# Attention on one core: values' low parts beside the high ones, and the two halves of the output bank added by VectorE

## The chip, the cores and the metric

One core of a Trainium2 chip runs the whole program. TensorE multiplies (PE in the profile; PEld is its weight load), ScalarE (ACT) and VectorE (DVE) empty the eight accumulation banks, GpSimd (POOL) works between on-chip tiles, SyncE's queue (SP) issues transfers. The metric is the device time in microseconds: 1926.93 us is the median of 3 runs of the kernel before (1922.9 to 1926.97).

## The reference, cut to what matters

The program is a small decoder on 2 batches of 512 tokens of width 512. Six stages follow each other: causal attention with 16 heads of 32 (`a0`), attention to a memory, a mixture of experts, rotary causal attention with 32 query heads and 8 key/value heads of 64 (`a1`), linear attention, and a second mixture. Only the two attentions change:

```
def _L0_attn_ref(x, Wq, Wk, Wv, Wo):            # NH = 16, hd = 32
    att = jnp.einsum('bhtd,bhsd->bhts', q, k) / jnp.sqrt(hd) + mask   # causal
    w = jax.nn.softmax(att, axis=-1)
    z = jnp.einsum('bhts,bhsd->bhtd', w, v)
    return z.transpose(0, 2, 1, 3).reshape(B, T, D) @ Wo.T

def _L1_attn_ref(x, w_in, w_out, rms_w):        # 8 groups of 4 heads, DQK = DV = 64
    q, k = _rope(q), _rope(k)
    attn = jax.nn.softmax(where(causal, qk, -inf), axis=-1)
    o = jnp.einsum('bghsp,bgxpd->bghsd', attn, v)
    return x + jnp.einsum('bsc,mc->bsm', o, w_out)
```

## The kernel before

**Precision.** Every f32 operand is held as two fp32r parts: a high part (ScalarE's rounding copy) and a low part (what VectorE or GpSimd gets by subtracting it, helper `low_part`, lines 158 to 165). A product is three passes of fp32r matmuls, high by high, high by low, low by high (helper `product`, line 153). The part low by low is left out.

**Slots.** Both attentions are one class, `Attention`. Each runs 4 steps of 128 output columns. In `a0` a step has 8 jobs (2 batches, 4 heads); in `a1` 16 (2 batches, 4 query tiles, 2 heads). A job is one head's softmax(QK)V over 512 tokens. The loop variable `m` counts slots, and each engine walks over them in its own order, which the program writes out by hand; semaphores tie them together. In slot `m` TensorE does the scores of job `m`, the transposes of the normalised weights of job `m-2`, a "fill", then the values of job `m-3` (`_pe_values`). VectorE does the masking and maximum of job `m` (line 836), the reciprocal of job `m-1` (line 842), the rotary work, the low part of job `m-2`'s transposed weights (`a_PHL`, three instructions on line 165), and its share of the fill.

**Fill.** The table `FILL` says which piece of a projection goes in a slot: `P` a projection of 12 matmuls, `T` the turning of the values, `O` a tile of the output product. In `a1` the fills repeat every 8 slots. I number them 0 to 7: P, P, P, OO, P, OO, P (of the values), T+P. An O of `a1` is 12 matmuls, one of `a0` 3. In `a0` 4 slots repeat, 0 to 3: P+OO, P, P, OOT. The first O of a slot 3, and of slot 7 in `a0`'s count of 8, reads the attention outputs of the job whose values were computed in the slot before.

**Rotary chain of `a1`.** A projected tile is emptied by ScalarE into `a_f` (line 809), turned by 4 transfers into `a_g` (line 669), multiplied by GpSimd (line 700) and VectorE (881), added (884), rounded (768), its low part taken (first instruction after the reciprocal two slots later, line 164 or 165), and moved by 4 transfers (line 654) into the operands of the scores. There are two `a_f`/`a_g` pairs, so the next projection but one waits for those moves.

**Output bank.** Bank 7 (`OB`) accumulates the values of all heads of a tile: 4 jobs in `a0`, 2 in `a1`. `VH` and `VL` hold the values' parts, head by head, each in its own columns of 128 with zeros elsewhere, so a head's product lands in its own partitions. After the last head ScalarE copies the bank into `QH` (line 759) and VectorE writes bank minus `QH` into `QL` (the end of its slot), both 128 partitions. `QL` then frees the bank and lets the O products start.

## Time and profile before

| | |
|---|---|
| median of 3 runs | 1926.93 us |
| profiled execution | 1936.33 us, of it span 1934.9 us |
| `a0`'s slots | about 40 to 245 us of the span |
| `a1`'s slots | about 979 to 1494 us |
| busy in the span | PE 94%, PEld 81%, DVE 58%, ACT 42%, POOL 52% |
| granted clock | 0.98 of 2.4 GHz |

A stretch of the page is only as slow as the wait that ends last in it, so the busy shares over the span say little about two stages that together fill some 37% of it (`a0`'s 205 us and `a1`'s 515 us of 1934.9). What is needed is which engine TensorE waits for inside a slot.

### The profile page before, as it was taken

How to read it: one execution, taken by the hardware profiler on the slowest of the kernel's cores; microseconds unless marked ns; L12 is line 12 of the kernel's file. 1: busy time of each engine (PE TensorE's matmuls, PEld its weight loads, DVE VectorE, ACT ScalarE, POOL GpSimd, SP SyncE). 2: the span in 40 equal slices, each digit the busy share in tenths (PEclk: the TensorE clock that was granted, in tenths of full speed). 3: DMA queues.
4: the chain of work that ended last, by engine and by line, in shares of the span. 5: the costliest groups of instructions: out<-in, count | busy, mean ns of one | idle time of the engine just before them, and what ended most of it. 6: DMA issues, size and time to landing. Idle time of an engine off the chain costs nothing.

```text
span 1934.9 us, 30810 instructions
## 1 busy us (share of the span) xinstructions
PE 1813.6 (94%) x10167; PEld 1568.5 (81%) x10167; DVE 1116.9 (58%) x2769; ACT 804.9 (42%) x2063; POOL 1009.1 (52%) x965
## 2 busy tenths in 40 slices
PE   7999989989799999999889999999999999999896
PEld 5888867778799999898668888888888888867795
DVE  6667785663233333335766666666665757566344
ACT  3766633222122222221257556665564433543231
POOL 3444342487773957895456556455453203116783
PEclk9999999999899999999999999999999999999998
DMA  3556430156553545544343243233321210012655
GB/s 116 171 154 202 138 136 35 58 182 220 179 181 132 197 161 179 188 153 118 90 115 93 66 105 103 56 89 98 80 69 55 73 50 1 24 49 98 207 199 191
DMA packets 104552, 232.54 MB, mean 120 GB/s; under 512 B 20673, under 2 KB 20929, under 8 KB 101329
## 3 DMA queue, kind: packets, MB, share of 16 engines
q1 hardware_dynamic: 84080, 144.31, 24.7%
q0 software_dynamic: 19744, 85.47, 13.4%
q8 instruction: 90, 1.47, 0.3%
q10 hardware_dynamic: 576, 0.79, 0.2%
q14 instruction: 62, 0.50, 0.1%
HBM read 126.23 MB, written 57.93 MB: 95 GB/s over the span
## 4 chain that ended last, share of the span: by engine, by line
PE 55%; DVE 5%; POOL 4%; issue 3%; DMA 3%; SPq 3%; ACT 2%; another core or an unknown queue 1%; POOLq 0%; DVEq 0%; ACTq 0%
PE bank L153 45%; PE bank L1025 2%; PE bank L1009 2%; PE bank L2188 2%; PE bank L2179 2%; SPq L669 1%; DMA a_g<-a_f 1%; POOL a_g L700 1%; SPq L654 1%; DMA a_QL<-a_g 1%; POOL f_UL L165 1%; POOL a_E L706 1%; DVE X L1894 1%; PE bank L2940 1%
## 5 line engine op out<-in xcount | busy, mean ns | idle before, releaser
L706 POOL TENSOR_SCALAR a_E<-a_E,a_inv 128x128 f32<-128x128 f32 (+3 forms) x384 | 222.1, 596 | 219.9 <-DVE a_inv L842 219.9
L153 PE MATMUL bank<-f_UH,f_XH 128*128 x596 | 200.8, 337 | 22.9 <-POOL f_UL L165 12.3
L739 ACT ACTIVATE a_E<-a_E,a_top 128x512 f32<-128x512 f32 (+3 forms) x384 | 211.1, 567 | 5.1 <-DVE a_top L836 5.0
L153 PE MATMUL bank<-f_UH,f_XL 128*128 x596 | 193.6, 325 | 0.0
L153 PE MATMUL bank<-f_UL,f_XH 128*128 x596 | 193.5, 325 | 0.0
L731 ACT ACTIVATE a_PHL<-bank 128x512 fp32r<-128x512 f32 (+1 forms) x288 | 131.0, 528 | 133.1 <-PE bank L1025 133.0
L153 PE MATMUL bank<-a_PHL,a_VH 128*128 128x512 f32 (+3 forms) x768 | 180.4, 324 | 0.3 <-DVE a_QL L165 0.3
L836 DVE CUSTOM_DVE_ANT_0 a_E<-a_causal,bank 128x512 f32<-128x512 bf16 (+3 forms) x384 | 163.8, 482 | 28.0 <-PE bank L1009 16.2
L1837 DVE TENSOR_TENSOR f_gate<-bank,f_gate 128x352 f32<-128x352 f32 x79 | 41.4, 525 | 206.6 <-PE bank L153 180.5
L165 DVE TENSOR_TENSOR a_PHL<-bank,a_PHL 128x512 fp32r<-128x512 f32 (+1 forms) x288 | 153.8, 588 | 10.1 <-ACT a_PHL L731 10.0
L1782 ACT ACTIVATE f_HH<-bank 128x256 fp32r<-128x256 f32 x220 | 59.9, 324 | 239.5 <-PE bank L2179 211.9
L700 POOL TENSOR_TENSOR a_g<-a_g,a_cos_sin 128x512 f32<-128x512 f32 x40 | 68.7, 1718 | 158.8 <-DMA a_g<-a_f 158.8
L153 PE MATMUL bank<-f_DH,f_HH 128*128 (+1 forms) x330 | 139.5, 423 | 9.9 <-issue 5.5
L153 PEld LDWEIGHTS bank<-a_PHL,a_VH 128*128 128x128 f32 x768 | 134.8, 189 | 14.3 <-DVE a_QL L165 0.6
L165 POOL TENSOR_TENSOR f_UL<-f_uraw,f_UH 128x2816 fp32r<-128x2816 f32 (+1 forms) x27 | 141.5, 5242 | 2.3
L1025 PE MATMUL bank<-ident,a_E 128*128 128x128 f32 x960 | 127.7, 278 | 14.9 <-DVE a_PHL L165 11.1
L153 PEld LDWEIGHTS bank<-f_UH,f_XH 128*128 128x128 f32 x596 | 113.4, 190 | 25.1 <-issue 25.1
L153 PE MATMUL bank<-f_DH,f_HL 128*128 (+1 forms) x330 | 131.6, 399 | 0.0
L153 PE MATMUL bank<-f_DL,f_HH 128*128 (+1 forms) x330 | 131.0, 397 | 0.0
L165 POOL TENSOR_TENSOR f_DL<-f_draw,f_DH 128x1024 fp32r<-128x1024 f32 (+1 forms) x54 | 98.3, 1839 | 61.4 <-DVE f_row L217 59.3
L1771 ACT ACTIVATE f_gate<-bank 128x352 f32<-128x352 f32 x110 | 51.2, 466 | 184.0 <-PE bank L153 151.1
L1025 PEld LDWEIGHTS bank<-ident,a_E 128*128 128x128 f32 x960 | 108.9, 142 | 21.7 <-DVE a_PHL L165 13.2
(407 smaller groups left out, 4954.3 us busy)
## 6 DMA issues: line engine op xcount, KB each, us to landing
f_uraw<-f_up POOLq DMA_DIRECT2D x18, 1408.0 KB
f_xb<-table SPq DMA_DIRECT2D x86, 256.0 KB
table<-f_ob SPq DMA_DIRECT2D x86, 256.0 KB
table<-a_zeros SPq DMA_DIRECT2D x31, 512.0 KB, 3.9
f_draw<-f_down POOLq DMA_DIRECT2D x27, 512.0 KB
a_g<-a_f SPq DMA_DIRECT2D x160, 64.0 KB, 2.0
a_raw<-a_qkv SPq DMA_DIRECT2D x36, 256.0 KB
f_uraw<-f_up POOLq DMA_DIRECT2D x9, 704.0 KB
```

What stands on the lines that cost most here:

```text
L153: m = pe.matmul(out, a, b, start=first and i == 0 and j == 0, stop=last and i == n - 1 and j == 2, skip_group_check=not check)
L165: return dve.tensor_tensor(lo, src, hi, ALU.subtract)
L700: e.tensor_tensor(g, g, self.cos_sin[:, 1, :], ALU.mult).then_inc(*self.s_p2.up(N, *x))
L706: e.tensor_scalar(self.E[sl][:, a], self.E[sl][:, a], self.inv[:, sl, i:i + 1], 0.0, ALU.mult, ALU.add).then_inc(*self.s_nrm.up(N, m - 1, i))
L731: e.activation(self.PH[m % 2][:, at:at + size], bank[:, 0:size], ACT.Copy).then_inc(*self.s_phi.up(N, m - 2, ci))
L739: x = e.activation(E, E, ACT.Exp, scale=-1.0, bias=self.top[:, sl, i:i + 1], accum_out=self.total[:, sl, i:i + 1])
L836: e.tensor_tensor_reduce(self.E[sl][:, self.E_AT[i]:self.E_AT[i] + w], self.causal[:, T - w:T], bank[:, off:off + w], -1.0, HUGE, ALU.add, ...
L1009: t = e.matmul(bank[:, off:off + w], (self.QH, self.QL)[h][:, r, qs], keys[:, h, ks], start=x == 0, stop=x == 1)
L1025: t = e.transpose(self.k.bank[bk][:, at:at + P], self.E[sl][:, self.E_AT[i] + sblk * P:self.E_AT[i] + (sblk + 1) * P], self.k.ident[:, :])
L1771: e.activation(self.gate[:, :], bank[2 + n % 2][:, 0:INNER], ACT.Silu).then_inc(*self.s_gate.up(N, n))
L1782: m = e.activation(self.HH[ps, cs, :], src, ACT.Copy)
L1837: e.tensor_tensor(self.gate[:, :], bank[4 + n % 2][:, 0:INNER], self.gate[:, :], ALU.mult).then_inc(*self.s_hid.up(N, n))
```

## The change

1. `VH` and `VL` become one tile `V`: a head's low part sits in the same 128 columns, 64 columns away from the high part. One pass then gives high-by-x in the head's own half of the bank's partitions and low-by-x in the other half. The values take two passes (`V` by `PH`, `V` by `PL`) instead of three. Low by low is now included.
2. The bank holds one half's heads at a time, so it closes after 2 jobs in `a0` and after every job in `a1`, and every opening waits until VectorE has emptied it.
3. Emptying is three instructions on 64 partitions: ScalarE copies the own half to `QH`; VectorE writes `S` = other half minus `QH` (the bank is read 64 partitions away from where `S` is written), waits for itself, and writes `QL` = own half plus `S`.
4. VectorE does this one slot later than before, behind the maximum and the reciprocal of the new slot.
5. `a0`'s fill puts `T` ahead of the two `O`. The clearing of `V` at the start falls from two tiles to one in `a0`, to none in `a1`.

```diff
@@ -439,7 +439,8 @@
         else:
             self.KH, self.KL = sb("KH", [heads, NTOK], F32R), sb("KL", [heads, NTOK], F32R)
             self.cos_sin = sb("cos_sin", [2, T])
-        self.VH, self.VL = sb("VH", [heads, NT, P], F32R), sb("VL", [heads, NT, P], F32R)
+        self.V = sb("V", [heads, NT, P], F32R)
+        self.S = sb("S", [T])
         self.E = [sb(f"E{i}", [1280]) for i in range(self.SLOTS)]
         PHL = sb("PHL", [4, 1280], F32R)
         self.PH, self.PL = [PHL[:, i, :] for i in range(2)], [PHL[:, 2 + i, :] for i in range(2)]
@@ -459,9 +461,9 @@
         if rotary is None:
             self.FIRST = [[("P", K, 0)], [("P", 0, 0)], [("P", V, 0)], [("T", 0)]]
             self.FILL = [[("P", K, 1), ("O", 2, -1), ("O", 3, -1)], [("P", 0, 1)], [("P", V, 1)],
-                         [("O", 4, -1), ("O", 5, -1), ("T", 1)],
+                         [("T", 1), ("O", 4, -1), ("O", 5, -1)],
                          [("P", K, 0, 1), ("O", 6, -1), ("O", 7, -1)], [("P", 0, 0, 1)], [("P", V, 0, 1)],
-                         [("O", 0), ("O", 1), ("T", 0, 1)]]
+                         [("T", 0, 1), ("O", 0), ("O", 1)]]
             self.SPLIT = {2: (K, 1), 3: (0, 1), 5: (V, 1), 6: (self.wt, 0)}
             self.LEAD = {K: 3, 0: 4, V: 2, self.wt: 2}
             self.NORM = {-2: [4, 5], -1: [6, 7]}
@@ -594,9 +596,9 @@
                 for i in range(TT):
                     self.s_nrm.plan((N, m, i))
                 self.s_av.plan((N, m))
-                if h == self.heads - 1:
-                    self.s_ohi.plan((N, j, r, b))
-                    self.s_olo.plan((N, j, r, b))
+                if self.closes(h):
+                    for s in (self.s_ohi, self.s_olo):
+                        s.plan((N, j, r, b, self.half(h)))
     def moves(self, j, c, b):
@@ -613,6 +615,25 @@
                     [(self.QL[up, c, a], f[dn, :]), (self.QL[dn, c, a], g[dn, :])]]
         return [[(self.KH[up, 0, a], g[up, :]), (self.KH[dn, 0, a], g[up, :]), (self.KL[up, 0, a], f[up, :])],
                 [(self.KH[up, 1, a], g[dn, :]), (self.KH[dn, 1, a], g[dn, :]), (self.KL[dn, 1, a], f[dn, :])]]
+    def half(self, h):
+        return h * self.hd // self.HALF
+    def opens(self, h):
+        return h * self.hd % self.HALF == 0
+    def closes(self, h):
+        return (h + 1) * self.hd % self.HALF == 0
+    def low_columns(self, cs):
+        at = (cs.start + self.HALF) % P
+        return slice(at, at + self.hd)
+    def halves(self, h):
+        own = slice(self.half(h) * self.HALF, (self.half(h) + 1) * self.HALF)
+        return own, slice((1 - self.half(h)) * self.HALF, (2 - self.half(h)) * self.HALF)
     def out_weights(self, x, r):
         return x[:, self.wt + r, :, :].rearrange("p k n -> p (k n)")
@@ -679,8 +700,8 @@
         else:
             e.memset(self.KL[:, :, :].bitcast(F32), 0.0)
         e.memset(self.causal[:, :], 0.0).then_inc(*self.k.g.up())
-        for z in (self.VH, self.VL):
-            e.memset(z[:, :, :, :].bitcast(F32), 0.0)
+        if 2 * self.hd < P:
+            e.memset(self.V[:, :, :, :].bitcast(F32), 0.0)
         last = self.causal[:, T - P:T]
         e.wait_ge(*self.k.g.now())
         e.affine_select(out=last, in_=last, compare_op=ALU.is_ge, fill=MASKED, base=0, pattern=[[-1, P]],
@@ -753,11 +774,13 @@
                     self.norm.act_tile(i)
             if self.rotary is not None and m == self.VALUES:
                 self._act_rotated(m - 1)
-            if 3 <= m < self.M + 3 and self.jobs[m - 3][3] == self.heads - 1:
+            if 3 <= m < self.M + 3 and self.closes(self.jobs[m - 3][3]):
                 j, b, r, h = self.jobs[m - 3]
+                own, other = self.halves(h)
+                bank = self.k.bank[self.OB]
                 e.wait_ge(*self.s_av.after(N, m - 3))
-                e.activation(self.QH[:, r, b * T:b * T + T], self.k.bank[self.OB][:, :], ACT.Copy).then_inc(
-                    *self.s_ohi.up(N, j, r, b))
+                e.activation(self.QH[own, r, b * T:b * T + T], bank[own, :], ACT.Copy).then_inc(
+                    *self.s_ohi.up(N, j, r, b, self.half(h)))
     def _act_rotated(self, m):
@@ -840,6 +863,8 @@
                 sl = (m - 1) % self.SLOTS
                 e.wait_ge(*self.s_ex.after(N, m - 1, 2))
                 e.reciprocal(self.inv[:, sl, :], self.total[:, sl, :]).then_inc(*self.s_inv.up(N, m - 1))
+            if 4 <= m < self.M + 4 and self.closes(self.jobs[m - 4][3]):
+                self._dve_low_values(m - 4)
             if self.rotary is not None:
                 for x in self.projected(m - 2):
                     s = self.slot[x]
@@ -859,12 +884,17 @@
                 self.norm.dve_second()
             for i in self.NORM.get(m, []):
                 self.norm.dve_rest(i)
-            if 3 <= m < self.M + 3 and self.jobs[m - 3][3] == self.heads - 1:
-                j, b, r, h = self.jobs[m - 3]
-                a = slice(b * T, b * T + T)
-                e.wait_ge(*self.s_ohi.after(N, j, r, b))
-                low_part(e, self.QL[:, r, a], self.k.bank[self.OB][:, :], self.QH[:, r, a]).then_inc(
-                    *self.s_olo.up(N, j, r, b))
+    def _dve_low_values(self, m):
+        e, N, (j, b, r, h) = self.k.dve, self.name, self.jobs[m]
+        (own, other), a, key = self.halves(h), slice(b * T, b * T + T), (N, j, r, b, self.half(h))
+        bank = self.k.bank[self.OB]
+        e.wait_ge(*self.s_ohi.after(*key))
+        e.tensor_tensor(self.S[own, :], bank[other, :], self.QH[own, r, a].bitcast(F32), ALU.subtract).then_inc(*self.k.d.up())
+        e.wait_ge(*self.k.d.now())
+        e.tensor_tensor(self.QL[own, r, a], bank[own, :], self.S[own, :], ALU.add).then_inc(*self.s_olo.up(*key))
     def _stats(self, loaded, tiles):
@@ -901,7 +931,7 @@
                 src, bs = bank[:, :].rearrange("p (i c) -> p i c", i=TT), slice(b * TT, b * TT + TT)
                 e.wait_ge(*self.s_vhi.after(N, j, b))
                 for h, cs in self.head_rows:
-                    i = low_part(e, self.VL[:, h, bs, cs], src[:, :, cs], self.VH[:, h, bs, cs], scale=1.0)
+                    i = low_part(e, self.V[:, h, bs, self.low_columns(cs)], src[:, :, cs], self.V[:, h, bs, cs], scale=1.0)
                 i.then_inc(*self.s_vlo.up(N, j, b))
             else:
                 _, j, g = x
@@ -979,7 +1009,7 @@
                 if g == 0:
                     e.wait_ge(*self.s_wlo.after(N, j, self.wt + Q - 1))
                 if g % TT == 0:
-                    e.wait_ge(*self.s_olo.after(N, j, self.queries[-1], g // TT))
+                    e.wait_ge(*self.s_olo.after(N, j, self.queries[-1], g // TT, self.half(self.heads - 1)))
                 a = slice(g * P, g * P + P)
                 product(e, bank[:, :], [(self.QH[:, r, a], self.QL[:, r, a]) for r in range(Q)],
                         [(self.out_weights(self.WH, r), self.out_weights(self.WL, r)) for r in range(Q)]).then_inc(
@@ -1033,19 +1063,18 @@
         j, b, r, h = self.jobs[m]
         if r == self.queries[0] and h == 0:
             e.wait_ge(*self.s_vlo.after(N, j, b))
-        if h == 0 and self.OB in emptied:
+        if self.opens(h) and self.OB in emptied:
             e.wait_ge(*emptied[self.OB])
         for ci, chunk in enumerate(self.TCHUNKS):
             e.wait_ge(*self.s_plo.after(N, m, ci))
             for sblk, _ in chunk:
                 a = slice(self.P_AT[sblk], self.P_AT[sblk] + T - sblk * P)
-                t = product(e, self.k.bank[self.OB][:, sblk * P:T],
-                            [(self.VH[:, h, b * TT + sblk, :], self.VL[:, h, b * TT + sblk, :])],
-                            [(self.PH[m % 2][:, a], self.PL[m % 2][:, a])],
-                            first=h == 0 and sblk == 0, last=h == self.heads - 1 and ci == 2)
+                for x, weights in enumerate((self.PH, self.PL)):
+                    t = e.matmul(self.k.bank[self.OB][:, sblk * P:T], self.V[:, h, b * TT + sblk, :], weights[m % 2][:, a],
+                                 start=self.opens(h) and sblk == 0 and x == 0, stop=self.closes(h) and ci == 2 and x == 1)
         t.then_inc(*self.s_av.up(N, m))
-        if h == self.heads - 1:
-            emptied[self.OB] = self.s_olo.after(N, j, r, b)
+        if self.closes(h):
+            emptied[self.OB] = self.s_olo.after(N, j, r, b, self.half(h))
     def projections_done(self):
```

VectorE's order in a slot 3 of `a1` (`a_top` is the running minimum, `a_inv` the reciprocal, `a_f` and `a_g` the rotary tiles). Before:

```order
L884 TENSOR_TENSOR a_f<-a_f,a_g 128x512
L165 TENSOR_TENSOR a_PHL<-bank,a_PHL 128x512 x2
L165 TENSOR_TENSOR a_PHL<-bank,a_PHL 128x256
L165 TENSOR_TENSOR a_QL<-bank,a_QH 128x512
L836 ISA a_E,a_top<-a_causal,bank 128x512
L836 ISA a_top 128x1
```

and, behind that slot's reciprocal:

```order
L842 RECIPROCAL a_inv<-a_total 128x4
L164 SCALAR_TENSOR_TENSOR a_f<-a_f,a_g 128x512
L881 TENSOR_TENSOR a_f<-a_f,a_cos_sin 128x512
L884 TENSOR_TENSOR a_f<-a_f,a_g 128x512
```

The same place in the changed kernel:

```order
L865 RECIPROCAL a_inv<-a_total 128x4
L895 TENSOR_TENSOR a_S<-bank,a_QH 64x512
L897 TENSOR_TENSOR a_QL<-bank,a_S 64x512
L164 SCALAR_TENSOR_TENSOR a_f<-a_f,a_g 128x512
L911 TENSOR_TENSOR a_f<-a_f,a_cos_sin 128x512
L914 TENSOR_TENSOR a_f<-a_f,a_g 128x512
```

What emptied the bank stood ahead of the slot's first maximum; now a pair of instructions stands behind the last one and the reciprocal, ahead of the rotary work, in every slot of `a1` and every second one of `a0`.

TensorE's order in a slot 3 of `a0`, from the transposes to the first values. Before:

```order
L1025 MATMUL bank<-ident,a_E 128x128 x10
L153 MATMUL bank<-a_WH,a_QH 128x512
L153 MATMUL bank<-a_WL,a_QH 128x512
L153 MATMUL bank<-a_WH,a_QL 128x512
L153 MATMUL bank<-a_WH,a_QH 128x512
L153 MATMUL bank<-a_WL,a_QH 128x512
L153 MATMUL bank<-a_WH,a_QL 128x512
L972 MATMUL bank<-ident,a_f 128x128 x4
L153 MATMUL bank<-a_PHL,a_VH 128x512 x2
L153 MATMUL bank<-a_PHL,a_VL 128x512
```

In the changed kernel:

```order
L1055 MATMUL bank<-ident,a_E 128x128 x10
L1002 MATMUL bank<-ident,a_f 128x128 x4
L153 MATMUL bank<-a_WH,a_QH 128x512
L153 MATMUL bank<-a_WL,a_QH 128x512
L153 MATMUL bank<-a_WH,a_QL 128x512
L153 MATMUL bank<-a_WH,a_QH 128x512
L153 MATMUL bank<-a_WL,a_QH 128x512
L153 MATMUL bank<-a_WH,a_QL 128x512
L1073 MATMUL bank<-a_PHL,a_V 128x512 x2
```

The four turnings of the values moved ahead of the two O, and the third pass of the values is gone.

## Rows read from the trace of the kernel before

**Rows 1.** Windows: one 4-slot group of `a0`, two 8-slot groups of `a1`.
```profile
core 0: us, PE busy (x) PEld busy (x) DVE busy (x) ACT busy (x) POOL busy (x), PEclk, DMA share, GB/s
100.55:126.69 26.14, 26.14 (x159) 23.34 (x158) 18.34 (x59) 18.37 (x55) 12.07 (x19) 1.00 0.52 159
1100.50:1165.06 64.56, 62.95 (x367) 55.67 (x365) 43.40 (x121) 39.59 (x110) 33.31 (x41) 1.00 0.34 87
1165.06:1230.40 65.34, 63.13 (x367) 55.64 (x365) 43.52 (x121) 39.72 (x110) 35.74 (x43) 1.00 0.33 85
```

**Rows 2.** Timeline (start us, duration us) of PE, `a1`: one job's values, next scores.
```profile
1105.63 0.62 PE L153 MATMUL bank<-a_PHL,a_VH 128*128 128x512 f32 x2
...
1107.53 0.39 PE L1009 MATMUL bank<-a_KH,a_QL 128*128 128x512 f32 x1
```

**Rows 3.** Timeline of PE, `a1`: slot 3, scores to first output product.
```profile
1121.59 0.39 PE L1009 MATMUL bank<-a_KH,a_QL 128*128 128x512 f32 x1
...
1123.67 0.64 PE L1025 MATMUL bank<-ident,a_E 128*128 128x128 f32 x3 [0.64 <-DVE a_PHL L165]
...
1125.52 0.47 PE L153 MATMUL bank<-a_WH,a_QH 128*128 128x512 f32 x1
```

**Rows 4.** Timeline of DVE in slots 1 to 3 of the same group.
```profile
1111.26 1.79 DVE L881 TENSOR_TENSOR a_f<-a_f,a_cos_sin 128x512 f32<-128x512 f32 x1
...
1116.99 0.65 DVE L164 SCALAR_TENSOR_TENSOR a_f<-a_f,a_g 128x512 fp32r<-128x512 f32 x1
1120.29 0.69 DVE L881 TENSOR_TENSOR a_f<-a_f,a_cos_sin 128x512 f32<-128x512 f32 x1 [2.65 <-DMA a_g<-a_f]
...
1122.94 1.61 DVE L165 TENSOR_TENSOR a_PHL<-bank,a_PHL 128x512 fp32r<-128x512 f32 x3
1124.68 0.69 DVE L165 TENSOR_TENSOR a_QL<-bank,a_QH 128x512 fp32r<-128x512 f32 x1
1125.29 0.68 DVE L836 CUSTOM_DVE_ANT_0 a_E<-a_causal,bank 128x512 f32<-128x512 bf16 x1
...
1127.01 0.66 DVE L164 SCALAR_TENSOR_TENSOR a_f<-a_f,a_g 128x512 fp32r<-128x512 f32 x1
```

**Rows 5.** Timeline of SyncE's queue and ACT: moves and turns, an emptying.
```profile
1111.37 0.50 SPq L654 DMA_DIRECT2D a_QH<-a_g  x1
...
1116.22 2.65 SPq L669 DMA_DIRECT2D a_g<-a_f  x4
1118.93 0.58 SPq L654 DMA_DIRECT2D a_QH<-a_g  x1
...
1115.60 0.60 ACT L809 ACTIVATE a_f<-bank 128x512 f32<-128x512 f32 x1 [1.11 <-DMA a_QL<-a_g]
```

**Rows 6.** Waits, 900 to 1380 us: total, times, longest.
```profile
DVE a_QL L165 <- ACT a_QH L759: 43.0, 21, 3.9
```

**Rows 7.** Timeline of PE and ACT, `a1`, slots 6 and 5.
```profile
1281.23 0.39 PE L1009 MATMUL bank<-a_KH,a_QH 128*128 128x256 f32 x1 [0.63 <-DVE X L913]
...
1148.11 0.63 ACT L781 ACTIVATE a_WH<-a_raw 128x512 fp32r<-128x512 f32 x1 [7.30 <-PE bank L153]
```

**Rows 8.** Timeline of PE and DVE, `a0`: slot 3 from its scores.
```profile
100.55 0.81 PE L1006 MATMUL bank<-a_KS,a_QS 96*128 96x512 f32 x4
...
102.22 0.47 PE L153 MATMUL bank<-a_WH,a_QH 128*128 128x512 f32 x1
...
106.04 0.89 PE L1006 MATMUL bank<-a_KS,a_QS 96*128 96x512 f32 x4
...
101.38 0.69 DVE L165 TENSOR_TENSOR a_QL<-bank,a_QH 128x512 fp32r<-128x512 f32 x1 [3.47 <-ACT a_QH L759]
```

**Rows 9.** Timeline of PE, end of `a1`: a slot without fill, last output product.
```profile
1458.48 0.39 PE L1009 MATMUL bank<-a_KH,a_QH 128*128 128x512 f32 x1
...
1462.79 0.40 PE L1009 MATMUL bank<-a_KH,a_QL 128*128 128x512 f32 x1
...
1493.03 0.47 PE L153 MATMUL bank<-a_WH,a_QH 128*128 128x512 f32 x1 [1.50 <-DVE a_QL L165]
```

More of the change, by code:

```diff
@@ L452, in __init__ @@
                          [self.E[i][:, a * D:(a + 1) * D] for i in range(self.SLOTS) for a in range(2)], rms)
+        self.HALF = P // 2
         self.head_rows = [(h, slice(h * hd, h * hd + hd)) for h in range(heads)]
@@ L796, in _act_fill @@
                 for h, cs in self.head_rows:
-                    i = e.activation(self.VH[:, h, b * TT:b * TT + TT, cs], src[:, :, cs], ACT.Copy, scale=1.0)
+                    i = e.activation(self.V[:, h, b * TT:b * TT + TT, cs], src[:, :, cs], ACT.Copy, scale=1.0)
                 i.then_inc(*self.s_vhi.up(N, j, b))
```

## The prediction, written before the changed kernel ran

> **What bounds the kernel now.** I read the page for the shares, then the windows of the attention stages, then the timelines of TensorE and VectorE over one repeating group of slots, and last those of ScalarE and SyncE's queue where one of the two waited. In a group of 4 slots of `a0` TensorE is busy for all of 26.14 us; in a group of 8 slots of `a1` for 62.95 of 64.56 us and 63.13 of 65.34 [rows 1]. The granted clock is 1.00 there, the level of 2.4 GHz. So TensorE sets the pace, and a pass taken from it is worth its full time wherever nobody else becomes late. VectorE is busy for 43.4 of 64.56 us, but that average hides the place that matters. In slot 3 of `a1` TensorE has the scores at 1121.59 and waits for VectorE's `a_PHL` before its transposes at 1123.67 [rows 3]. VectorE is late there: its maximum starts at 1125.29 [rows 4], 3.7 us behind the scores. It is late because its rotary work waited 2.65 us for a transfer (`a_g`) [rows 4]. The reader is to see that two things run side by side in `a1`: TensorE's stream, and a chain of transfers and VectorE steps that catches up with it once per group.
>
> **What the change removes.** The values of a job take 12 matmuls from 1105.63 to 1107.53, 1.90 us [rows 2]. All passes are alike, so the third of them is 1.90 / 3 = 0.63 us. There are 96 jobs (32 in `a0`, 64 in `a1`): 61 us if all of it counted. The clearing of `V` at the start saves GpSimd time only, ahead of its first weights; the first slots wait for the norm on VectorE, so I put it at nothing.
>
> **What it adds.** VectorE gets 160 instructions in place of 40. One of 512 columns from the bank takes 0.69 us alone and lets the next begin after 0.61 (`a_QL` at 1124.68, the next at 1125.29) [rows 4]. The trace has none on 64 partitions, and none whose input lies in other partitions than its output; the columns are the same 512, so I take the same 0.69. The second waits for the first: 0.69 + 0.03 + 0.69 = 1.41 us to the result, 1.32 until the next instruction. From below, two overlapped instructions would be 0.61 + 0.69 = 1.3. From above, the longest VectorE instruction of 512 columns here is the rotary product at 1111.26, 1.79 us while GpSimd works on the partner tile [rows 4]: twice that is 3.6 us. I take 1.41, since the rows that read the bank are the nearest. ScalarE gets 40 more copies of 0.60 us; it waits 1.11 us in the same slot for a transfer [rows 5], which hides them.
>
> **What it moves.** The old `a_QL` stood at the end of a slot, waiting for ScalarE's copy of values just computed: 43.0 us of waiting in 21 times [rows 6]. That wait goes. The new pair stands behind the maximum and reciprocal. It rarely waits itself, because ScalarE's copy is from the slot before. But three others wait for it. (a) The first O of slot 3 or 7. (b) The next opening of the bank. (c) Everything behind it on VectorE: the low part that releases SyncE's moves, the rotary product, `a_PHL`.
>
> **(a) in `a1`.** `a_PHL`'s three end for the next instruction at 1122.94 + 1.53 = 1124.47; without the old `a_QL` the maxima start there. From 1125.29 to 1127.01 maxima and reciprocal take 1.72 us [rows 4]. Then the pair, 1.41, and 0.15 to reach TensorE (`a_QL` ended at 1125.37, the O began at 1125.52 [rows 3, 4]): 1124.47 + 1.72 + 1.41 + 0.15 = 1127.75, where the O now starts at 1125.52. That is 2.2 us later than before, although TensorE was ready earlier: what it saved in slots 0 to 2 (3 x 0.63) is lost as well, because `a_PHL` hangs on the transfer chain. Other groups give 1.7 to 2.0; I take 1.95. After it the values of slots 3 to 7 save 5 x 0.63 = 3.15. Net per group: 3.15 - 1.95 = 1.2 us.
>
> **(c) in `a1`.** The pair stands before the low part of slot 1 and slot 2. In slot 1 what is removed pays for it: the old instruction, 0.61, and its wait, 43.0 / 21 = 2.0 us on average [rows 6], against 1.32. In slot 2 the low part ended at 1117.6 (started at 1116.99) [rows 4] and would now end at 1118.9. Its move was issued at 1118.93 in any case, since the queue was busy with the turns, 1116.22 + 2.65 = 1118.87 [rows 5]. So the chain isn't late by it, but there is no slack left. If that cover is gone, the chain is 1.3 us longer per group: 10 us over 8 groups. The rotary product of slot 2 waits 2.65 us for its transfer [rows 4], which hides the pair once more.
>
> **One more loss in `a1`.** In slot 5 of every second group ScalarE waits 7.30 us, until TensorE is through with its O, before it rounds new output weights [rows 7]; VectorE's addition to `X` in that slot hangs on it, and the third score matmul group of slot 6 waits 0.63 us for that addition [rows 7]. The shorter values only lengthen this wait: 0.63 lost in those groups.
>
> **(a) in `a0`.** Slot 3 started at 100.55 and took 5.49 us; its O began at 102.22 without waiting, since `a_QL` was early [rows 8]. Now: a 512-column matmul is 512 / 3840 x 1.90 = 0.25 us [rows 2], so the first maximum comes 0.25 + 0.15 = 0.4 us after the scores begin (in `a1`, two passes, 0.65); then 1.72, 1.41 and 0.15: the O at 3.7 us. The two O are 6 x 0.25 = 1.5, the values 1.27: 6.45 instead of 5.5, +0.95. Slots 0 to 2 save 0.63 each (their openings come later in the slot than the pair). Net per group 1.9 - 0.95 = 0.95 us.
>
> **(b) at the ends.** A slot without a P or O has nothing between transposes and values. In `a1` such a slot took 1462.79 - 1458.48 = 4.31 us [rows 9]; now the pair is done 0.65 + 1.72 + 1.41 + 0.15 = 3.9 us after the scores, and with values of 1.27 it takes 5.2: +0.9 each. The last group of `a1` has three of them, then three jobs in which TensorE, ScalarE and VectorE take turns on one bank (values 1.3, copy 0.6, pair 1.4) before the last O, which now starts at 1493.03 [rows 9]. The last group with its end: +1.3 for the O of slot 3, -1.3 for the values of the two slots with O, +2.7 for the three empty ones, +0.7 for the taking turns: +3.4. That of `a0`: +0.95 for slot 3, +1.2 for the empty slot that opens the bank, -1.3 for two that don't, +0.85 in the last two openings: +1.7.
>
> **The sum.** `a0`: first group, three slots at -0.63, -1.9; five groups at -0.95, -4.75; the last with its end +1.7: -4.9. `a1`: first group (no O, bound by the chain but for two slots) -1.3; three groups with the weight wait 3 x (1.2 - 0.63) = -1.7; three without, 3 x 1.2 = -3.6; the last +3.4: -3.2. Together -8.1 us. The profiled execution took 1936.33 us (1934.9 of it span), 9.4 more than the median of the runs. It would take 1928.2, and the median falls from 1926.93 to 1918.8. Of 61 us taken from TensorE, over 50 come back as waits.
>
> **A rule that speaks against the pair.** Successive instructions of VectorE start 0.61 us apart at a duration of 0.69 [rows 4], so they overlap by 0.08. The Trainium skill ("VectorE: DVE Perf Modes", section "Two Vector instructions with no wait between them") says that an instruction is held until all earlier ones have finished when its input starts in another 32-partition group than the last input from that memory. No run here shows this yet. Here it would hold the first of the pair behind the reciprocal, and for the upper half the maximum after it: 0.1 us at each of some 20 places where TensorE waits for the pair. By it the sum is -6.1 instead of -8.1 us.
>
> **Rivals.**
> *Covered.* The old wait of VectorE for ScalarE [rows 6] is what makes it late, and without it VectorE runs ahead: then the O waits 0 to 1 us and the savings of slots 0 to 2 hold. Against it: in slots 1 and 2 the wait is for a transfer [rows 4, 5]. It gives up to 8 x 0.63 - 1.2 = 3.8 us more per group of `a1` and 0.95 of `a0`; with half of the first, in six groups each, 11 + 6 = 17 us more, 25 in all: 1902. With no wait at all, 61 us: 1866.
> *Nothing.* The openings cost in ordinary slots as well: a P slot has scores (1.27), transposes and 12 x 0.25 = 3.0 of projection ahead of its values, over 4.3 us, and the pair at 3.9 if VectorE is on time. When it is a microsecond behind, the values wait too. With 0.5 us in one slot of each of the 16 groups it takes 8 us, the whole gain: 1927.
> *Slower.* The rotary chain. Its place is the low part behind the pair in slots 1 and 2; its price 1.3 us each, where SyncE's queue does not hide it; it decides once the low part is later than the end of the turns, for which there is 0.0 us of slack today [rows 5]. Both in all 8 groups: 8 x 2.6 = 21 us, less 8.1: 1940. It also comes if the pair costs its upper bound (2.2 us more at about 20 places, 44 us: 1963).
> *Not what it says.* If reading across partitions needed another route, VectorE's instruction at L895 would show it as a longer duration; this is part of the case above.
>
> **Chances.** Forecast 0.52; covered 0.17 (of it 0.04 for the full 61 us); nothing 0.13; slower 0.18. A difference of 0.2% (4 us) is about what a measurement of this kernel tells from none. The forecast reaches from 1909 to 1925, by the bounds of the pair (0.1 us of it moves the sum by 2 us) and my reading of one group for all; nearly all of it is faster. From covered 0.17, forecast 0.49 and 0.04 of the others, faster is 0.70; same 0.14; slower 0.16. The range is 1899 to 1933: it leaves out the full gain and most of the slower case.
>
> **What would show it.** TensorE's matmuls of the values: 768, two per width, 1.27 us a job. In slot 3 of both stages a wait of TensorE for L897 ahead of the first O, 1.4 to 2.5 us; in slots 0 to 2 of `a1` no gain, in 4 to 7 0.63 each. L895 and L897 at 0.69 us. VectorE's wait for ScalarE's `a_QH` nearly gone. The group of `a0` at 25.2 us, those of `a1` at 63.4 to 64.8. The forecast is wrong if the groups shrink by 4 us or more (covered), or if moves and turns on SyncE's queue come later than before, measured from the group's start (slower).

## The result: slower by 1.45%

The changed kernel takes 1953.8 us (median of 6 runs, 1945.45 to 1959.1), the kernel before 1926.12 in the same job (6 runs, 1922.9 to 1928.69). The ratio is 1.0145 with a 95% interval of 1.012 to 1.017: 27.7 us slower, where I had forecast 8.1 us faster. The profiled execution took 1954.1 us, only 17.8 more than that of before. The profile of before is slow at its end: from the last O of `a1` to the end of the program, where the code is the same, it took 441.9 us, against 430.9 to 437.9 in the twelve other profiles of this case (433.5 in after). From `a1`'s first scores to its last O the change costs 28.4 us in the profiles, near the 27.7 of the medians.

### The profile page after: what moved, and what is told of

The parts are those of the page before. It is cut to its first block and busy times, and to the rows that moved or that the text cites. A ratio compares the mean times of both kernels' runs of the same rounds, so it can differ in the third digit from the quotient of the medians.

```text
span 1952.8 us, 30233 instructions
## 1 busy us (share of the span) xinstructions
PE 1778.7 (91%) x9777; PEld 1532.4 (78%) x9783; DVE 1211.1 (62%) x2889; ACT 831.5 (43%) x2103; POOL 1009.0 (52%) x962
## 5 line engine op out<-in xcount | busy, mean ns | idle before, releaser
L727 POOL TENSOR_SCALAR a_E<-a_E,a_inv 128x128 f32<-128x128 f32 (+3 forms) x384 | 230.6, 618 | 222.7 <-DVE a_inv L865 222.7
L153 PE MATMUL bank<-f_UH,f_XH 128*128 x596 | 200.9, 337 | 20.2 <-POOL f_UL L165 15.1
L1073 PE MATMUL bank<-a_PHL,a_V 128*128 128x512 f32 (+3 forms) x768 | 141.2, 327 | 14.5 <-DVE a_QL L897 14.5
L1073 PEld LDWEIGHTS bank<-a_PHL,a_V 128*128 128x128 f32 x768 | 128.6, 193 | 31.5 <-DVE a_QL L897 17.0
L153 PE MATMUL bank<-YH,a_WH 128*128 128x512 f32 x288 | 121.4, 421 | 6.3 <-ACT a_f L832 2.3
```

Source lines behind the costliest of these rows:

```text
L153: m = pe.matmul(out, a, b, start=first and i == 0 and j == 0, stop=last and i == n - 1 and j == 2, skip_group_check=not check)
L727: e.tensor_scalar(self.E[sl][:, a], self.E[sl][:, a], self.inv[:, sl, i:i + 1], 0.0, ALU.mult, ALU.add).then_inc(*self.s_nrm.up(N, m - 1, i))
L1073: t = e.matmul(self.k.bank[self.OB][:, sblk * P:T], self.V[:, h, b * TT + sblk, :], weights[m % 2][:, a], start=self.opens(h) and sblk == ...
```

## The profile after

**Stages.** The windows of the kernel after (columns as in [rows 1]): a group of `a0` from slot 3 to slot 3 as in [rows 1], two groups of 8 slots of `a1`, and slots 2 and 3 of the first of them.

```profile
98.27:123.72 25.45, 23.92 (x143) 21.05 (x141) 20.72 (x62) 19.07 (x56) 12.02 (x19) 1.00 0.53 166
1101.85:1170.50 68.65, 61.73 (x334) 53.48 (x333) 53.54 (x133) 41.67 (x113) 34.59 (x41) 0.95 0.33 81
1170.50:1237.25 66.75, 61.76 (x334) 53.63 (x333) 52.46 (x133) 43.16 (x115) 37.25 (x43) 0.95 0.33 83
1117.49:1125.58 8.09, 8.09 (x39) 7.37 (x39) 5.67 (x16) 4.92 (x14) 2.21 (x3) 0.79 0.39 94
1125.58:1140.16 14.58, 11.22 (x53) 9.04 (x51) 11.44 (x23) 5.86 (x15) 7.52 (x10) 0.88 0.44 106
```

The group of `a0` is 25.45 us; counted from slot 0 the regular ones take 25.2 to 25.5 us and one 26.45 (forecast 25.2). Those of `a1` are 68.65 and 66.75 instead of 64.56 and 65.34 [rows 1]; I had said 63.4 to 64.8. The same rows say how the loss is paid. Two passes instead of three save TensorE 8 x 0.63 = 5.06 us in a group. In the first group its idle time grows from 64.56 - 62.95 = 1.6 to 68.65 - 61.73 = 6.9 us, which is +5.3. Its busy time should fall from 62.95 to 57.9 but falls only to 61.73, which is +3.8, at a granted clock of 0.95 instead of 1.00. 5.3 + 3.8 - 5.06 = 4.1, the difference of the two lengths. In the second group: +2.8, +3.7, -5.06, in sum +1.4. So the loss has two parts, waiting and slower work. The slow stretches are slots 2 and 3: 0.79 and 0.88.

For the whole of `a1`, from the start of its first scores to the start of its last O, before and after:

```profile
979.33:1493.03 513.70, 489.44 (x2818) 429.24 (x2816) 340.24 (x960) 311.87 (x868) 269.92 (x337) 0.99 0.33 84
```
```profile
977.12:1519.26 542.14, 474.77 (x2562) 407.50 (x2560) 416.95 (x1056) 333.27 (x901) 279.03 (x337) 0.94 0.31 79
```

Idle time: 24.3 becomes 67.4, +43.1. Busy time: 489.4 less 64 x 0.63 = 40.3 would be 449.1 and is 474.8, +25.6. Sum: 43.1 + 25.6 - 40.3 = 28.4, the difference of the two lengths. The slower work is over a third of what eats the saving.

**Who waits.** The waits of TensorE in that stretch, first after, then before (us in total, times, longest).

```profile
PE bank L153 <- DVE a_QL L897: 17.0, 8, 2.2
PE bank L1039 <- DMA a_QH<-a_f: 14.4, 8, 2.3
PE bank L1055 <- DVE a_PHL L165: 12.0, 8, 2.4
PE bank L1073 <- DVE a_QL L897: 10.1, 8, 2.1
PE bank L1039 <- DVE X L943: 8.7, 6, 2.1
```
```profile
PE bank L1025 <- DVE a_PHL L165: 11.1, 9, 3.1
...
PE bank L1009 <- DMA a_QH<-a_f: 3.3, 2, 2.3
PE bank L153 <- DVE a_QL L165: 2.7, 4, 1.5
PE bank L1009 <- DVE X L913: 1.9, 3, 0.6
```

The first row is the wait I forecast (the O of slot 3 for the pair). The second I did not: the scores of slot 2 now wait in every group for the moved `QH`, before in two. The fourth is the opening of the bank; all but one of its places are in the last group of `a1`. The fifth is slot 6's wait for the addition to `X`. These four grew by 42 us, nearly all of the 43.1.

**TensorE, slots 2 and 3** of the group of rows 3 to 5 (start us, duration us; slot 0 begins at 1101.85).

```profile
1117.49 0.52 PE L1039 MATMUL bank<-a_KH,a_QH 128*128 128x512 f32 x1 [1.70 <-DMA a_QH<-a_f]
...
1119.72 2.00 PE L1055 MATMUL bank<-ident,a_E 128*128 128x128 f32 x10
...
1125.58 0.40 PE L1039 MATMUL bank<-a_KH,a_QL 128*128 128x512 f32 x1
...
1132.00 0.77 PE L153 MATMUL bank<-a_WH,a_QH 128*128 128x512 f32 x1 [2.22 <-DVE a_QL L897]
1132.57 0.63 PE L153 MATMUL bank<-a_WL,a_QH 128*128 128x512 f32 x1
1132.99 0.63 PE L153 MATMUL bank<-a_WH,a_QL 128*128 128x512 f32 x1
...
1135.02 0.40 PE L153 MATMUL bank<-a_WL,a_QH 128*128 128x512 f32 x1
1135.26 0.39 PE L153 MATMUL bank<-a_WH,a_QL 128*128 128x512 f32 x1
```
```profile
1132.00:1134.70 2.70, 2.70 (x7) 2.12 (x7) 2.67 (x3) 0.68 (x4) 2.44 (x3) 0.50 0.69 168
1134.70:1138.90 4.20, 4.20 (x20) 3.48 (x18) 2.56 (x5) 0.63 (x1) 1.92 (x3) 0.98 0.58 141
```

Behind the wait of 2.22 us the O matmuls start 0.43 us apart until 1134.7, at a granted clock of 0.50 (the level of 1.2 GHz), then 0.23 us apart at 0.98 (nearly all at 2.4). Six matmuls lose 0.2 us each. Before, the first O started with no such wait [rows 3]. This is the mildest of such places: from the first to the last of slot 3's 24 O matmuls the seven groups take 6.7 to 8.0 us, six of them before 5.3 and the last 6.0.

**VectorE, slots 1 to 3**, and the transfers and ScalarE's emptying beside it.

```profile
1112.23 0.17 DVE L865 RECIPROCAL a_inv<-a_total 128x4 f32<-128x4 f32 x1
1112.43 0.68 DVE L895 TENSOR_TENSOR a_S<-bank,a_QH 64x512 f32<-64x512 f32 x1
1113.15 0.69 DVE L897 TENSOR_TENSOR a_QL<-bank,a_S 64x512 fp32r<-64x512 f32 x1
1113.87 0.69 DVE L164 SCALAR_TENSOR_TENSOR a_f<-a_f,a_g 128x512 fp32r<-128x512 f32 x1
...
1128.62 0.67 DVE L859 CUSTOM_DVE_ANT_0 a_E<-a_causal,bank 128x512 f32<-128x512 bf16 x1
...
1130.24 0.17 DVE L865 RECIPROCAL a_inv<-a_total 128x4 f32<-128x4 f32 x1
1130.44 0.68 DVE L895 TENSOR_TENSOR a_S<-bank,a_QH 64x512 f32<-64x512 f32 x1
1131.16 0.69 DVE L897 TENSOR_TENSOR a_QL<-bank,a_S 64x512 fp32r<-64x512 f32 x1
```
```profile
1114.59 0.50 SPq L675 DMA_DIRECT2D a_QH<-a_g  x1
...
1120.12 2.67 SPq L690 DMA_DIRECT2D a_g<-a_f  x4
```
```profile
1119.49 0.60 ACT L832 ACTIVATE a_f<-bank 128x512 f32<-128x512 f32 x1 [1.79 <-DMA a_QL<-a_g]
```

Read it as a chain. The low part of slot 1 starts 12.0 us after the group's first scores (1113.87 - 1101.85). Its move is issued the moment it is done, at 12.7, where it was 10.9 before (1111.37 - 1100.50 [rows 1, 5]). In slot 2 the move still waits for the turns on the queue (1120.12 + 2.67), as I had said, so that low part isn't on the chain. The emptying that waits for the moves starts at 17.6 instead of 15.1, the maxima of slot 3 at 26.8 instead of 24.8 [rows 4], and the first O at 30.15 instead of 25.0 [rows 3]. The pair takes 1.64 us from the reciprocal's start to the low part's; without it the low part starts 0.09 us behind the reciprocal.

This group is the latest of the seven that have O products. In five of them the low part of slot 1 starts at 11.3 us (before 10.2 in all seven) and its move is issued at 12.0 (before 10.9), so the wait of slot 2 is there in all. But the maxima of slot 3 come at 25.3 us on average of the seven, after as before. What is late in every group is the O behind them: it starts 3.4 us after the first maximum, since maxima, reciprocal and pair stand ahead of it, where before it started 0.2 to 1.0 us after it. In the six full groups that makes it 3.1 us late on average.

## The experiments

The numbers are medians; each kernel shares its job with runs of the kernel before (1926.78, 1926.46 and 1925.25 us in the three jobs), and the ratio is to those.

**Only `a0`.** In `a1` the values' two tiles, the whole bank and the single instruction at the end of the slot are as before.

```diff
+        self.whole = rotary is not None
     def closes(self, h):
-        return (h + 1) * self.hd % self.HALF == 0
+        return h == self.heads - 1 if self.whole else (h + 1) * self.hd % self.HALF == 0
```

> Only a0 is changed (two passes, pair one slot later, T ahead of the O); a1 is as before. Theory A (the whole loss is in a1, where the pair lengthens the rotary chain): a0 keeps what its slots show, about 5 us, so 1926 - 5 = 1921 (1919 to 1923), and a1 starts earlier but takes its old 64.4 to 65.3 us a group. Rival (the change also costs outside a1, through the tail of the program or SyncE's queue): at or above 1926.

1926.95 us, ratio 1.001 (0.9996 to 1.0025). So the loss is in `a1`. But the 5 us of `a0` aren't there either; see below.

**Low part first.** In `a1` the pair stands behind the rotary low part.

```diff
-            if 4 <= m < self.M + 4 and self.closes(self.jobs[m - 4][3]):
+            mine = 4 <= m < self.M + 4 and self.closes(self.jobs[m - 4][3])
+            if mine and self.rotary is None:
                 self._dve_low_values(m - 4)
             if self.rotary is not None:
                 for x in self.projected(m - 2):
                     ...
+            if self.rotary is not None and mine:
+                self._dve_low_values(m - 4)
```

> The kernel after, but in a1 VectorE writes the rotary low part (which releases SyncE's moves) ahead of the pair instead of behind it; a0 unchanged. Theory A (the pair ahead of the low part lengthens the rotary chain): in slots 1 and 2 the low part comes 1.5 us earlier, the scores of slot 2 no longer wait 1.70 us for a_QH, the maxima and the O of slot 3 come 1.4 to 2.8 us earlier; 1.7 to 2.8 us in each of 8 groups, 14 to 22 us: 1932 to 1940. Rival B (the late first O alone, the pair standing behind the maxima of slot 3): in slot 3 nothing moves, 1952 to 1954. Rival C (TensorE's clock falls after waits): half of A's gain goes with the wait of slot 2, about 1945.

1942.29, ratio 1.0087 (1.0069 to 1.0104): 11.5 us back for changing the order of VectorE's work, with the same instructions. Here are VectorE's slot 2 and the first O of slot 3 in this kernel, whose slot 0 begins at 1098.97.

```profile
1116.74 0.17 DVE L865 RECIPROCAL a_inv<-a_total 128x4 f32<-128x4 f32 x1
1116.83 0.66 DVE L164 SCALAR_TENSOR_TENSOR a_f<-a_f,a_g 128x512 fp32r<-128x512 f32 x1
1117.53 0.69 DVE L899 TENSOR_TENSOR a_S<-bank,a_QH 64x512 f32<-64x512 f32 x1
```
```profile
1127.10 0.50 PE L153 MATMUL bank<-a_WH,a_QH 128*128 128x512 f32 x1 [2.81 <-DVE a_QL L901]
...
1130.38 0.59 PE L153 MATMUL bank<-a_WH,a_QL 128*128 128x512 f32 x1
1130.81 0.40 PE L153 MATMUL bank<-a_WH,a_QH 128*128 128x512 f32 x1
```

TensorE's wait for the moved `QH` falls from 14.4 us in `a1` to 6.0. The O still waits, 2.81 us, since the pair in slot 3 now has one more instruction ahead of it, and behind it eight matmuls start 0.42 to 0.43 us apart. Theory A holds in direction, but it had said 14 to 22 us. The waits for the pair grew meanwhile (at the O from 14.8 to 18.1 us, at the openings from 4.5 to 11.2, both between 979 and 1500 us of the span); that this is the missing part is argued, not shown.

**One step.** In `a1` the pair is one instruction; the sum in the other half of the bank is left out of the result.

```diff
-        e.tensor_tensor(self.S[own, :], bank[other, :], self.QH[own, r, a].bitcast(F32), ALU.subtract)...
-        e.wait_ge(*self.k.d.now())
-        e.tensor_tensor(self.QL[own, r, a], bank[own, :], self.S[own, :], ALU.add)...
+        e.tensor_tensor(self.QL[own, r, a], bank[own, :], self.QH[own, r, a].bitcast(F32), ALU.subtract)...
```

> The kernel after, but in a1 VectorE's pair is one instruction of 64 partitions (own half minus the high part); the other half's sum, the values' low part by the high weights, is left out. It shows what the second VectorE instruction costs. Theory A: 0.7 to 0.8 us less at two places of the chain and once ahead of the first O, 1.4 to 2.2 us a group: 11 to 18 us, 1936 to 1943. Rival B (only what stands between the maxima of slot 3 and the O counts): 0.75 us a group and at 4 openings of the end, 9 us: 1945. Rival D (the pair costs far more than its records, through the partition shift): over 20 us, below 1934.

1934.69, ratio 1.0035 (1.0022 to 1.0048): 19.1 us less than after, a little over A's 18 and far over B's 9. It is also close to where rival D begins (20), a pair that costs more than its records; the records show no such cost, since `S` and `QL` take 0.68 and 0.69 us. Per removed instruction of 0.72 us that is 0.3 us at each of 64 jobs, though TensorE waits directly for the pair at 16 places only. This fits a chain. Even one instruction would not have paid in this place, ahead of the low part and of the O.

**Idle matmuls in the waits.** 6 ahead of the scores of slot 2, 8 ahead of the first O of slot 3, into the bank that is used next.

```diff
+                if g % TT == 0 and self.rotary is not None:
+                    self.k.warm(8, bk)
                 if g % TT == 0:
                     e.wait_ge(*self.s_olo.after(...))
...
+        if self.rotary is not None and m % 8 == 2:
+            ...
+            self.k.warm(6, self.score_bank[m, 0])
```

> The kernel after, but in a1 TensorE does idle matmuls of 512 columns during its two new waits, into the bank that it is about to use: 6 ahead of the scores of slot 2 and 8 ahead of the first O of slot 3. Rival C (a third to a half of the loss is TensorE's clock after those waits): the O of slot 3 run at 0.23 us a matmul instead of 0.43 (6 of them, 1.2 us) and the transposes of slot 2 take 1.25 instead of 2.0; 1 to 2 us a group, 8 to 16 us: 1938 to 1946, with the granted clock of a1 at 0.98 or more. Theory A alone: the chain runs in its own time, the matmuls only fill a wait, 1952 to 1956.

1943.63, ratio 1.0086 (1.0073 to 1.0099): 10.2 us back by work that computes nothing. The same O in this kernel:

```profile
1129.08 3.15 PE L140 MATMUL bank<-identb 128*128 128x512 bf16 x8
1131.88 0.58 PE L153 MATMUL bank<-a_WH,a_QH 128*128 128x512 f32 x1
1132.29 0.39 PE L153 MATMUL bank<-a_WL,a_QH 128*128 128x512 f32 x1
1132.52 0.40 PE L153 MATMUL bank<-a_WH,a_QL 128*128 128x512 f32 x1
```
```profile
979.00:1500.00 521.00, 475.37 (x2635) 399.05 (x2634) 406.43 (x1039) 327.95 (x891) 276.91 (x336) 0.98 0.32 83
```

The O matmuls start 0.23 us apart from the second on, and `a1`'s clock is 0.98 instead of 0.94. In all seven groups slot 3's 24 O matmuls now take 5.3 to 5.4 us. The earliest O of a group is still 28.2 us into it, as in after (28.3). So the time comes back behind the O, and the slow matmuls of slot 2 cost little, since a wait follows them. Theory C holds, beside A.

**Early.** As low part first, and in slot 3 the pair stands ahead of the maxima.

```diff
+            if self.rotary is not None and m % 8 == 3 and 4 <= m < self.M + 4:
+                self._dve_low_values(m - 4)
             if 0 <= m < self.M:
                 ...                                  # the four maxima
...
-            if self.rotary is not None and mine:
+            if self.rotary is not None and mine and m % 8 != 3:
                 self._dve_low_values(m - 4)
```

> As low_first, and in slot 3 of a1 the pair stands ahead of the four maxima. Theory B (the O of slot 3 waits for the maxima and reciprocal that stand ahead of the pair, 1.72 us): the wait of TensorE ahead of the O falls from 2.8 to about 1.1 us, 1.7 us in each of 8 groups and up to 0.5 more from TensorE's clock: 14 to 18 us under low_first's 1942.3, 1925 to 1929. Rival (the chain sets the group's end, not the O: the delayed maxima make slots 4 and 5 wait instead): 1938 to 1944.

1924.87, ratio 0.9986 (0.997 to 1.0002): 17.4 us less than low part first. The two places of the pair are together worth 28.9 us, as much as the whole loss against before.

**Early alone**, with the pair otherwise ahead of the low part as in after (the upper part of the diff above; the pair's condition behind the reciprocal leaves out slot 3).

> The kernel after, and only in slot 3 of a1 the pair stands ahead of the maxima; in the other slots it stands ahead of the low part as in after. If the two moves of the pair act at different waits (O of slot 3; moved Q of slot 2), their gains add: 1953.8 - 17.4 (early against low_first) = 1936. If the late maxima of slot 3 are the one bound for both, moving the pair ahead of them gives less than 10 us: 1944 to 1950.

1937.15, ratio 1.0063 (1.0044 to 1.0081): 16.7 us under after. Within the few us by which the medians here can be told apart, the gains add (11.5 + 16.7 = 28.2 against 28.9 together): two waits at two places.

**Early with idle matmuls**, 3 and 6 of them.

> As early, and TensorE does idle matmuls in its waits in a1: 3 ahead of the scores of slot 2, 6 ahead of the first O of slot 3. Theory C (a wait of about 2 us costs TensorE's clock for the 6 to 9 matmuls behind it, 1.2 to 1.7 us a time) and B together: another 5 to 10 us under early, 1916 to 1922, below the kernel before. Rival (the remaining waits are too short to cost clock): the same as early within 3 us.

1921.16, ratio 0.9975 (0.9963 to 0.9988): faster than the kernel before by 5.3 us. It is 3.7 us under early, between the two expectations (5 to 10, or within 3), and the two intervals overlap; so the times don't show this last gain. The granted clock of `a1` rises from 0.97 to 0.99. Slot 3 and the group of 8 slots:

```profile
1096.01:1159.61 63.60, 60.94 (x343) 51.57 (x342) 52.89 (x133) 41.55 (x113) 33.77 (x41) 1.00 0.36 88
1117.05:1128.99 11.94, 10.94 (x59) 8.67 (x58) 10.90 (x23) 6.00 (x15) 7.63 (x10) 1.00 0.50 124
```

Slot 3 is 11.94 us instead of 14.58, at a clock of 1.00. The group is 63.6 us, inside what I had forecast for after, though this kernel reaches it by other orders and by idle matmuls.

**A third pass.** In `a1` the pass with the low part of the weights is done twice, so that part counts double. This takes TensorE's saving there back, and everything else of after stays.

```diff
-                for x, weights in enumerate((self.PH, self.PL)):
+                for x, weights in enumerate((self.PH, self.PL, self.PL) if self.rotary is not None else (self.PH, self.PL)):
```

> The kernel after with a third pass in the values of a1 (the low weights' pass twice, so the low part of the weights counts double): TensorE's saving is taken back there, and the pair, the openings and the order stay. Theory A (slots 7 to 3 of a1 are set by the rotary chain, TensorE's saving only lengthens its waits): 0.63 us in slots 4, 5, 6 and the start of 7 alone, 8 x 2 to 2.5 = 16 to 20 us more than after: 1970 to 1974; less if the pass shortens waits and so keeps the clock up: down to 1962. Rival (TensorE sets the pace in all slots, and the pair only adds fixed waits): 64 x 0.63 = 40 us more, 1994.

1975.78, ratio 1.026 (1.0241 to 1.0278): 22.0 us over after, for passes of 40 us. So about 18 us of what the change takes from TensorE in `a1` brought nothing there. This is a little over theory A's 16 to 20 and far from the rival's 40.

**The pair in the old place**, at the end of the slot of its values.

```diff
-            if 4 <= m < self.M + 4 and self.closes(self.jobs[m - 4][3]):
+            if self.rotary is None and 4 <= m < self.M + 4 and self.closes(self.jobs[m - 4][3]):
                 self._dve_low_values(m - 4)
...
+            if self.rotary is not None and 3 <= m < self.M + 3:
+                self._dve_low_values(m - 3)
```

> The kernel after, but in a1 the pair stands where the old single instruction stood, at the end of the slot of its values, waiting for ScalarE's copy. If the move one slot later was the harm: the O of slot 3 starts as in the kernel before (no wait), and the group loses only the second instruction at each end of a slot: 0.9 us in slots 1, 2 and 3 against before's place, less 4 x 0.63 saved: about 65 us a group, 1925 to 1932. If the pair itself in the chain is the harm, wherever it stands: VectorE waits 2.0 us more for ScalarE in 21 places, 1945 to 1960.

1954.97, ratio 1.0152 (1.0132 to 1.0173), the same as after. VectorE's waits for ScalarE's copy are back (57.0 us, 53 times), the low part of slot 1 comes at 11.1 to 11.9 us into the group and the O of slot 3 at 26.5 to 29.6, much as in after. So a slot later was not in itself the harm; the old place, with this pair in it, is no better.

**`a0` early too.** Early with idle matmuls, and in `a0`'s slot 3 the pair ahead of the maxima as well.

```diff
-            if self.rotary is not None and m % 8 == 3 and 4 <= m < self.M + 4:
+            if m % (4 if self.rotary is None else 8) == 3 and 4 <= m < self.M + 4:
```

> As early_warm, and in a0 too the pair stands ahead of the four maxima in slot 3 of every 4, where VectorE waits 2.44 us for the scores today. The O there waits 1.50 us for the pair and the next is a slot of 5.75 to 6.57 us. If the O is what holds TensorE: slot 3 takes 5.2 instead of 6.57, 7 x 1.3 = 9 us: 1912. Rival (the maxima, now 1.4 us later, hold the weights of job m and the transposes two slots on, which have little slack in a0's short slots): 1918 to 1924, no gain.

1923.78, ratio 0.9994 (0.9984 to 1.0005): no gain, and 2.6 us over the kernel without it (the intervals overlap a little). Slot 3 falls from 6.57 to 5.79 us, slot 0 behind it grows from 7.16 to 8.4: its scores stop in the middle for the values' low parts, which VectorE now does later.

```profile
107.02 0.99 PE L1048 MATMUL bank<-a_KS,a_QS 96*128 96x384 f32 x3 [0.73 <-DVE a_V L164]
```

**`a0` as before**, `a1` as in early with idle matmuls.

```diff
+        self.whole = rotary is None
...
-                         [("T", 1), ("O", 4, -1), ("O", 5, -1)],
+                         [("O", 4, -1), ("O", 5, -1), ("T", 1)],
```

> As early_warm in a1, and a0 as in the kernel before (three passes, whole bank, O ahead of T). It measures a0's part a second time. If a0's change gives what its slot starts show (about 2 us): 1923. If it gives nothing, as a0_only's 1926.95 against 1926.78 says: 1921. If my 4.9 us were right: 1926.

1920.15, ratio 0.997 (0.9957 to 0.9983), the best, though not to be told from the 1921.16 with `a0` changed. By two pairs of kernels the change in `a0` gives nothing that can be measured.

## Why the prediction was wrong

**What TensorE saves** was right: 768 matmuls of values, 1.26 us a job. The pair was nearly right: forecast 1.41 us to the result, measured 1.41 and 0.20 to begin behind the reciprocal.

The sum was wrong in `a1`. By the starts of the scores in TensorE's timeline (us, after less before):

| part of `a1` | forecast | measured |
|---|---|---|
| first group | -1.3 | +0.9 |
| the six groups between | -5.3 | +19.8 |
| last group with its end | +3.4 | +7.8 |
| together | -3.2 | +28.4 |

One of the six takes 3.3 us more on average: +3.1 up to the first O (forecast +1.95), +1.3 from there to the end of slot 3 (forecast -0.63), -1.0 in slots 4 to 7 (forecast -2.5, of which the weight wait was to take 0.63 in every second group).

**The step that failed first is "(c) in `a1`"**, "So the chain isn't late by it, but there is no slack left", priced at nothing. It looked at the low parts of slots 1 and 2 alone. For slot 1 it let "its wait, 43.0 / 21 = 2.0 us on average" pay for the pair. In the group of the rows the old instruction waited 0.70 us there, in the other six 0.42 to 0.71; the long waits that make the average lay at the ends of slots 4 and 6. Rows of VectorE before, ends of slots 0, 4 and 6:

```profile
1108.36 0.69 DVE L165 TENSOR_TENSOR a_QL<-bank,a_QH 128x512 fp32r<-128x512 f32 x1 [0.70 <-ACT a_QH L759]
...
1140.84 0.69 DVE L165 TENSOR_TENSOR a_QL<-bank,a_QH 128x512 fp32r<-128x512 f32 x1 [3.27 <-ACT a_QH L759]
1158.44 0.69 DVE L165 TENSOR_TENSOR a_QL<-bank,a_QH 128x512 fp32r<-128x512 f32 x1 [2.55 <-ACT a_QH L759]
```

So in slot 1 0.61 + 0.70 = 1.3 us went and 1.64 - 0.09 = 1.55 came. The larger part it left out: the pair of slot 0 stands ahead of that slot's rotary product, where only a transfer wait of 0.42 us hides some of it. Before, the product waited for its transfer and started 2.89 us into the group. After, in five of seven groups, it waits for no transfer and starts at 3.85, as soon as `QL` lets it; here the second group, which begins at 1170.50:

```profile
1103.39 0.69 DVE L881 TENSOR_TENSOR a_f<-a_f,a_cos_sin 128x512 f32<-128x512 f32 x1 [0.42 <-DMA a_g<-a_f]
```
```profile
1173.02 0.69 DVE L895 TENSOR_TENSOR a_S<-bank,a_QH 64x512 f32<-64x512 f32 x1
1173.74 0.68 DVE L897 TENSOR_TENSOR a_QL<-bank,a_S 64x512 fp32r<-64x512 f32 x1
1174.35 0.67 DVE L911 TENSOR_TENSOR a_f<-a_f,a_cos_sin 128x512 f32<-128x512 f32 x1
```

That is 1.0 of the 1.1 us by which the low part of slot 1 is late. In the group shown above it starts at 4.57 instead, behind a transfer, and the low part is 1.8 us late. TensorE then waits 1.7 us for the moved `QH` in slot 2. In the same group of low part first the low part is back at 10.1 us (1109.07 - 1098.97), and that was worth 11.5 us; the product of slot 0 stays late in it, and no run moves the pair behind that product. The mechanism stood among the rivals ("The rotary chain", 0.18), though for slots 1 and 2 only; in kind it is what happened.

**(a) in `a1`** had the right mechanism and a short size. The forecast took 0.8 us off the maxima of slot 3 for the removed instruction and its wait; on average they came no earlier than before. That, and 0.1 for the pair's start behind the reciprocal, is most of what lies between +1.95 and +3.1. Early, which takes the pair out from behind the maxima, gave back 17.4 us.

**A term was missing: TensorE's clock.** I priced a wait at its length. The work behind it then ran at half pace for a while, 25.6 us more of busy time in `a1`. The idle matmuls gave back 10.2 us without an earlier start of the O. This is part of why that rival's 1940 was too low: it had no such term.

**(b)** was right at an empty slot: 5.36 us against 5.2 (openings at 1499.12 and 1504.48). **The weight wait** was not what I took it for. ScalarE's wait for the weights did not grow (21.9 us before, 22.0 after, 3 times each). TensorE's wait for `X` in slot 6 did, from 1.9 us in three groups to 8.7 in six, about 1.1 us a group where I had 0.63 in every second. That may be most of what slots 4 to 7 lack; what makes `X` late is not told apart.

**(a) in `a0`.** Most groups came out near 25.2 us, slot 3 at 6.57 (6.45). Still the sum of -4.9 isn't there. By the starts of the slots' scores `a0`'s first to last slot take 187.1 us in after, against 188.8 before: -1.7. Against my terms the first group with O gave 0.9 instead of 1.9, one slot 3 took 7.57 us, the other groups gave 0.8 instead of 0.95, and the last slots lost 2.2 instead of 1.7. Ten profiles with this change show 186.1 to 187.7, the two with `a0` as before 188.8 and 189.5, so some 2 us are saved there. The times of the kernel with `a0` alone allow from 0.8 us less to 4.8 us more than before (its interval). Whether the 2 us arrive can't be told: between `a0`'s last slot and `a1`'s first scores the same code took 753.3 to 756.4 us in twelve profiles and 749.7 in one, more than the effect.

**The rule on held instructions.** The trace agrees with the Trainium skill ("VectorE: DVE Perf Modes", section "Two Vector instructions with no wait between them"). Behind the reciprocal `S` starts 0.20 us after it (1130.24 to 1130.44), where the low part starts after 0.09 (1116.74 to 1116.83 in low part first). Behind `QL` the next instruction starts after 0.72 us when the input moves from the upper half (1113.15 to 1113.87), and after 0.61 when it doesn't (`QL` at 1121.39 in slot 2, `L164` at 1122.00). That is 0.1 us at each place, as I had taken it. No run measures what it costs in all; my estimate was 2 us, far less than what went wrong.

**The chances.** 0.70 for faster rested on an average of waits set against the rows of one place. The range, cut off at 1933, left out even the 1940 of the rival that came nearest in kind. The 1963 beside it lies nearer to 1953.8 only by luck: it supposed a pair of 3.6 us, and the pair took 1.41.

## What to carry to other kernels

Where TensorE waits once per group for a chain of other engines, go through every link of it before placing a new step, also those that start in the slot before: here a step of 1.4 us cost less behind a link, or ahead of the work that its own consumer doesn't need. Ask what a wait was at the very place, not on average. Price a new wait of TensorE at its length plus the matmuls behind it that may run at the lower clock, and compare the place of a step before the number of its instructions: here two moves of one pair were worth 28.9 us, and all the passes saved in `a1` were worth 22.

## What the runs showed of the hardware

- A wait of 1.70 us ahead of slot 2's scores was followed by a slot at a granted clock of 0.79. Waits of 1.47 to 2.23 us ahead of slot 3's O made its 24 matmuls take 6.7 to 8.0 us instead of 5.3. The wait alone does not decide: in `a0` one of 1.50 us was followed by matmuls at 0.23 us from the second on, and in early one of 1.20 us cost nothing while one of 0.70 us in another group was followed by some ten slow matmuls. The work ahead differs between these places.
- Idle matmuls in such a wait took the slow stretch on themselves: eight in 2.8 us at a granted clock of 0.55, and the useful ones behind them ran at 0.23 us and 1.00.
- VectorE reading the bank 64 partitions away from where it writes took 0.68 us for 512 columns on 64 partitions, as long as the aligned one on the same 64 (0.69) and the old one on 128 (0.69 [rows 4]). Half the partitions saved nothing.
